# An adaLN block on one core: a new program order on all five engines, the second token half's attention moved among the first feed-forward units, and the output bias folded into the output weights

## The reference

```python
mod = (silu(c) @ wmod).reshape(1, 6, 1, 256)     # c (1, 256)
sa, ca, ga, sb, cb, gb = mod[:, 0], ..., mod[:, 5]
ga, gb = sign(g) * maximum(abs(g), 0.25)         # each
h = layernorm(x) * (1 + ca) + sa                 # x (1, 1024, 256)
x = x + ga * attn(h)
h = layernorm(x) * (1 + cb) + sb
x = x + gb * ffn(h)

def attn(h):
    c = (h @ W_to_kv.T) @ W_compress.T           # 256 -> 64 -> 32
    ch = layernorm(c) * ln_gamma + ln_beta
    q, k, v = ch @ W_q_comp.T, *split(ch @ W_kv_comp.T)
    q, k = rope(q), rope(k)                      # one head of 32
    o = softmax(causal(q @ k.T / sqrt(32))) @ v
    z = o @ W_comp2lat.T
    return z @ W_to_kv + z @ W_out_res.T + b_out_res

def ffn(h):                                      # weights in 4-bit codes with scales
    Wg, Wu, Wd = dequant(...)                    # 2048 x 256 twice, 256 x 2048
    gate, up = h @ Wg.T, h @ Wu.T
    return (gelu_tanh(gate) * up) @ Wd.T
```

## Time and profile before

| | us |
|---|---|
| median of 3 runs | 225.3 |
| lowest, highest | 224.9, 228.08 |
| the profiled execution | 225.71 |
| its span, first to last instruction | 223.9 |
| PE, DVE, POOL, ACT busy in it | 201.6, 138.9, 105.2, 90.6 |
| mean granted TensorE clock, share of 2.4 GHz | 0.942 |

### The profile page before, as it was taken

One profiled execution on the slowest core, in us unless ns is written; L12 is line 12 of the kernel. 1 busy time (PEld: TensorE's weight loads), 2 busy tenths in 40 slices (PEclk: granted clock), 3 DMA queues, 4 the chain that ended last, 5 costly groups with the idle time before them and its releaser, 6 DMA issues. The chain is left out here.

```text
span 223.9 us, 3085 instructions
## 1 busy us (share of the span) xinstructions
PE 201.6 (90%) x1064; PEld 161.6 (72%) x1064; DVE 138.9 (62%) x249; ACT 90.6 (40%) x151; POOL 105.2 (47%) x78
## 2 busy tenths in 40 slices
PE   7998998799867984989999999997989999999991
PEld 2494596584545872868888988886778888888891
DVE  1656864938979789999999512575953333333234
ACT  2001321434176842544364356542343543543320
POOL 4412314506050666496996994660606515515200
PEclk9976975579999999999999999999999999999997
DMA  6999775400000000000000000000020000000002
GB/s 190 329 315 203 181 220 190 162 18 3 0 0 1 0 0 3 1 0 0 1 3 0 0 3 0 0 0 3 0 95 0 0 0 0 3 0 0 0 1 94
DMA packets 5645, 11.31 MB, mean 50 GB/s; under 512 B 544, under 2 KB 2752, under 8 KB 5632
## 3 DMA queue, kind: packets, MB, share of 16 engines
q1 hardware_dynamic: 5216, 10.82, 16.6%
q10 hardware_dynamic: 416, 0.33, 0.5%
HBM read 10.09 MB, written 1.05 MB: 50 GB/s over the span
## 5 line engine op out<-in xcount | busy, mean ns | idle before, releaser
L865 PE MATMUL ps<-H,WS 128*128 128x512 f32 x384 | 95.4, 395 | 8.6 <-DVE wmod_sb L721 5.7
L865 PEld LDWEIGHTS ps<-H,WS 128*128 128x128 f32 x384 | 69.6, 188 | 24.8 <-DVE wmod_sb L721 7.8
L865 PEld LDWEIGHTS ps<-WS,IS 128*128 128x128 f32 x384 | 49.8, 191 | 3.2 <-issue 1.1
L865 PE MATMUL ps<-WS,IS 128*128 128x256 f32 x384 | 51.0, 283 | 0.5 <-DVE wmod_sb L721 0.3
L417 ACT ACTIVATE IS<-wmod_sb 128x512 fp32r<-128x512 f32 x32 | 20.2, 632 | 69.4 <-PE ps L865 39.7
L514 POOL TENSOR_TENSOR WS<-wbuf,WS 128x1024 fp32r<-128x1024 f32 x16 | 39.1, 2441 | 9.8 <-ACT WS L398 9.8
L721 DVE TENSOR_TENSOR wmod_sb<-ps,wmod_sb 128x512 f32<-128x512 f32 x32 | 22.0, 688 | 31.8 <-PE ps L865 25.7
L519 POOL TENSOR_TENSOR WS<-wbuf,WS 128x512 fp32r<-128x512 f32 x16 | 22.4, 1402 | 39.8 <-ACT WS L405 39.8
L282 DVE TENSOR_TENSOR IS<-wmod_sb,IS 128x512 fp32r<-128x512 f32 x18 | 12.8, 710 | 24.4 <-ACT IS L417 23.6
L282 POOL TENSOR_TENSOR IS<-wmod_sb,IS 128x512 fp32r<-128x512 f32 x14 | 21.3, 1529 | 13.7 <-ACT IS L417 11.0
L411 ACT ACTIVATE wmod_sb<-ps 128x512 f32<-128x512 f32 x32 | 18.7, 584 | 5.8 <-PE ps L865 5.8
(11 more groups left out here) (116 smaller groups left out, 209.3 us busy)
## 6 DMA issues: line engine op xcount, KB each, us to landing
wbuf<-packed SPq DMA_DIRECT2D x8, 384.0 KB
wbuf<-scales SPq DMA_DIRECT2D x8, 384.0 KB
xres<-x SPq DMA_DIRECT2D x2, 512.0 KB, 6.2
wmod_sb<-wmod SPq DMA_DIRECT2D x1, 1024.0 KB, 10.4
out<-xres SPq DMA_DIRECT2D x4, 256.0 KB, 2.2
wmod_sb<-wmod SPq DMA_DIRECT2D x1, 512.0 KB, 7.3
rope_sb<-rope SPq DMA_DIRECT2D x1, 512.0 KB, 10.9
cst<-consts SPq DMA_DIRECT2D x1, 322.0 KB, 5.0
```

Source lines behind the costliest of these rows:

```text
L865: return pe.matmul(o, lhsT, rhs, start=start, stop=stop)
```

## The change

Nothing that is computed changes but the places of two factors: the first norm's rsqrt is multiplied in `compress`, behind `project_c`, instead of in `norm1` (now `center1`, which only subtracts the mean); and the bias row is accumulated into the output weights' product on PE, weighted so that it is multiplied by the softmax denominator and divided by it again. `add_bias`, `wsum`, `gab` and the broadcast load of the bias go. x is loaded in three parts, `consts` in two. `full_h0` goes from DVE to ACT, behind both pieces of `H`; the strided read of `norm2` goes into `transpose2`. `residual1` waits for all of its four tiles and interleaves the statistics of the second norm. In the core of the diff below, `for n` is the loop over units.

```diff
 # ACT
 norm1_out(0)
+gate_out()                     # the gb copy, waits for gb_done
 take_bytes(0); v_high(0); qk_high(0); norm1_out(1); take_bytes(1); max_rows(0); exps(0, 0, HT); out_high(0)
+gamma_beta1()                  # the second half's, from DVE
+split_gu(0, 0)
 v_high(1)
-take_bytes(2)
-split_gu(0, 0)
 split_d(0, 0)
 qk_high(1)
-...; max_rows(1)
-exps(1, 0, H0_BLOCK)
 stage_h0()                     # now with both pieces of hfull
-exps(1, H0_BLOCK, 2 * HT - 1); take_bytes(3); split_gu(1, 1); exps(1, 2 * HT - 1, 2 * HT); split_d(1, 1)
 for n in range(UNITS + 2):
-    G = n // 2 + 1
-    if n % 2 == 0 and G > 1: (take_bytes(G + 2)); split_gu(G, G % GROUPS)
+    G = (n + 1) // 2
+    if n % 2 == 0 and n // 2 + 2 < GROUPS: take_bytes(n // 2 + 2)
+    if n % 2: split_gu(G, G % GROUPS)
     gelu(n, n % 2, n >= 2)
-    if n == 0: out_high(1)
     inter_hi(n, n % 2, n >= 2)
-    if n % 2 and G > 1: split_d(G, G % GROUPS)
+    if n % 2: split_d(G, G % GROUPS)
+    if n == 2: max_rows(1); exps(1, 0, 2)
+    elif n == 3: exps(1, 2, 4)
+    elif n == 4: exps(1, 4, 6)
+    elif n == 5: exps(1, 6, 8)
+    elif n == 6: out_high(1)
 # POOL
 low_gu(0, 0, 0); low_d(0, 0, 0); rsqrt(N_LN2)
-for b in range(1, 2 * HT, 2): probs_low(pool, 1, b, b + 1)
-low_gu(1, 1, 1); low_d(1, 1, 1)
 for n in range(POOL_UNITS):
+    G = (n + 1) // 2
+    if n % 2: low_gu(G, G % 2, G)
+    if n == 3: probs_low(pool, 1, 1, 2)
+    elif n == 5: probs_low(pool, 1, 5, 6)
     inter_low(pool, n, n % 2, n >= 2)
+    if n == 3: probs_low(pool, 1, 3, 4)
+    elif n == 5: probs_low(pool, 1, 7, 8)
+    if n % 2: low_d(G, G % 2, G)
...
 # DVE
-    return STEPS_AT_START + 5 * n // 2
+    return 5 * max(0, n - 1) // 2
...
+decode(0)
+probs_low(dve, 0, 0, HT)
 compress(1)
+out_stack(0)
 normc(1)
+residual1(0)
 rotate(1)
 split_v(1)
+norm2(0, range(HT))
 split_qk(1)
+h_low(0, (0, 1))
+decode(1, 0, 3)
 for n in range(UNITS + 2):
     inter_full(n, n % 2, n >= 2)
...
+    if n == 0: decode(1, 3); row_max(1, 0, 4)
+    elif n == 1: row_max(1, 4, len(pieces(1)))
+    elif n == 3: probs_low(dve, 1, 0, 1); probs_low(dve, 1, 2, 3)
+    elif n == 4: probs_low(dve, 1, 4, 5)
+    elif n == 5: probs_low(dve, 1, 6, 7)
+    elif n == 7: out_stack(1)
+    elif n == 8: residual1(1)
+    elif n in (H1_UNIT - 2, H1_UNIT - 1): norm2(1, ...)
     elif n in (H1_UNIT + 1, H1_UNIT + 2): h_low(1, (n - H1_UNIT - 1,))
     decode_more(steps_before(n), steps_before(n + 1))
 # PE
-stay_warm(WC_B, 14)
+stay_warm(WC_B, 10)
...
+project_c(0, (0, 1))
 products(bank(WC_B)[:, 64:64 + DC], ...).then_inc(bias_done, 1)
-project_c(0)
+project_c(0, (2, 3))
 products(bank(GA_B, D), ...).then_inc(ga_done, 1)
-stay_warm(3, 4)
+mod_columns(..., SB, True); mod_columns(..., CB, True).then_inc(modb_done, 1)
 transpose_c(0)
-stay_warm(0, 3)
+products(bank(GB_B, D), ...).then_inc(gb_done, 1)
 project_qkv(0); stack_qk(0); transpose1(1)
-stay_warm(0, 2)
 scores(0, 0, HT)
-(mod_columns SB, CB); project_c(1); max_rows(0); key_scores(0, 0..1); transpose_c(1); key_scores(0, 2, 2)
-attend(0, 0, 0); key_scores(0, 3, 3); stay_warm(4, 3); attend(0, 1..3); project_qkv(1); output(0)
-stay_warm(6, 3); stack_qk(1); stay_warm(4, 10); scores(1, 0, 8); (gb products); max_rows(1); stay_warm(4, 4)
-for b, k in blocks(1): (key_scores, attend, transpose2(0), gate_up(0)); gate_up(1); (last attends)
+project_c(1, (0,)); max_rows(0); project_c(1, (1,)); key_scores(0, 0..2); project_c(1, (2,))
+key_scores(0, 3, 3); attend(0, 0..3); project_c(1, (3,)); stay_warm(4, 2); output(0); stay_warm(4, 2)
+transpose_c(1); project_qkv(1); stay_warm(6, 4); stack_qk(1); transpose2(0)
+gate_up(0, ...); scores(1, 0, 4); gate_up(1, ...); scores(1, 4, 8)
 for n in range(2, UNITS + 3):
     gate_up(n, ...)
-    if n == 2: output(1)
+    if n == 2: max_rows(1)
+    elif n == 3: attend(1, 0, HT); key_scores(1, 3, HT + 3)
+    elif n == 4: attend(1, 2, HT + 2); key_scores(1, 5, HT + 5)
+    elif n == 5: attend(1, 4, HT + 4); key_scores(1, 7, HT + 7)
+    elif n == 6: attend(1, 6, HT + 6)
+    elif n == 7: output(1)
     elif n == H1_UNIT: transpose2(1)
     down(n - 2, ...)
+    if n == 2: key_scores(1, 0..2)
+    elif n == 3: attend(1, 1, HT + 1); key_scores(1, 4, HT + 4)
+    elif n == 4: attend(1, 3, HT + 3); key_scores(1, 6, HT + 6)
+    elif n == 5: attend(1, 5, HT + 5)
+    elif n == 6: attend(1, 7, HT + 7)
```

More of the change, by code:

```diff
@@ L368, in stage_h0 @@
                 for e in range(2):
[L369 to L370 removed]
                     act.activation(H[:, 0, 0, e, :], bank(e), ACT.Identity, bias=mods[:, M_SB + e:M_SB + e + 1],
                                    scale=mods[:, M_CB + e:M_CB + e + 1]).then_inc(h_hi, 1)
+                act.wait_ge(c_done, 2)
+                for e in range(2):
+                    act.activation(hfull[:, e, :], bank(e), ACT.Identity, bias=mods[:, M_SB + e:M_SB + e + 1],
+                                   scale=mods[:, M_CB + e:M_CB + e + 1]).then_inc(h_full, 1)
             def stage_h1(e):
@@ L833, in _ @@
                     inter_low(dve, n, n % 2)
-                if n in (1, 2):
-                    residual1(1, (2 * n - 2, 2 * n - 1))
-                elif n == 3:
-                    stats2(1)
-                elif n in (H1_UNIT - 3, H1_UNIT - 2):
-                    first = 2 * (n - H1_UNIT + 3)
+                if n == 0:
+                    decode(1, 3)
+                    row_max(1, 0, 4)
+                elif n == 1:
+                    row_max(1, 4, len(pieces(1)))
+                elif n == 3:
+                    probs_low(dve, 1, 0, 1)
+                    probs_low(dve, 1, 2, 3)
+                elif n == 4:
+                    probs_low(dve, 1, 4, 5)
+                elif n == 5:
+                    probs_low(dve, 1, 6, 7)
+                elif n == 7:
+                    out_stack(1)
+                elif n == 8:
+                    residual1(1)
+                elif n in (H1_UNIT - 2, H1_UNIT - 1):
+                    first = 2 * (n - H1_UNIT + 2)
                     norm2(1, (first, first + 1))
@@ L1087, in _ @@
             attend(0, 3, 3)
+            project_c(1, (3,))
+            stay_warm(4, 2)
+            output(0)
+            stay_warm(4, 2)
+            transpose_c(1)
             project_qkv(1)
[L1089 to L1090 removed]
+            stay_warm(6, 4)
             stack_qk(1)
[L1092 to L1107 removed]
+            transpose2(0)
+            gate_up(0, 0, 0, 0, 0, first=True, later=False)
+            scores(1, 0, 4)
+            pe.wait_ge(h_full, 2)
             gate_up(1, 0, 0, 0, 1, later=False)
[L1109 to L1110 removed]
+            scores(1, 4, len(pieces(1)))
             for n in range(2, UNITS + 3):
[L1114 removed]
+                gate_up(n, n // 2, n // UNITS, n // 2 % 2, n % 2, first=n == UNITS)
                 if n == 2:
+                    max_rows(1)
+                elif n == 3:
+                    attend(1, 0, HT)
+                    key_scores(1, 3, HT + 3)
+                elif n == 4:
+                    attend(1, 2, HT + 2)
+                    key_scores(1, 5, HT + 5)
+                elif n == 5:
+                    attend(1, 4, HT + 4)
+                    key_scores(1, 7, HT + 7)
+                elif n == 6:
+                    attend(1, 6, HT + 6)
+                elif n == 7:
                     output(1)
@@ L1120, in _ @@
                 down(d, d // 2, d // UNITS, d // 2 % 2, d % 2, first=d % UNITS == 0, last=d == UNITS - 1)
+                if n == 2:
+                    for b in range(3):
+                        key_scores(1, b, HT + b)
+                elif n == 3:
+                    attend(1, 1, HT + 1)
+                    key_scores(1, 4, HT + 4)
+                elif n == 4:
+                    attend(1, 3, HT + 3)
+                    key_scores(1, 6, HT + 6)
+                elif n == 5:
+                    attend(1, 5, HT + 5)
+                elif n == 6:
+                    attend(1, 7, HT + 7)
             with pe.Fori(0, 3) as it:
```

345 lines of the change are left out of this document (152 added, 193 removed).

## The result

The changed kernel takes 250.69 us (median of 4 executions, 249.61 to 252.95) against 225.1 us: 1.11 times as long, 95% interval 1.099 to 1.124. Its profiled execution took 251.63 us, 25.9 more than that of before.

The account below looks back on a forecast made before the run. PE, busy 90%, was taken as nearly saturated only from gate_up(14), after a front chain of small steps and a middle with waits. Front 59.5 + middle 96.15 + rest 81.7 + tail 4.6 + 1.8 = 243.8 us (median 243), range 225 to 256.

Parts of the forecast that it names:

- rsqrt queued behind both low parts, ends 57.2: Front, POOL: second norm's rsqrt waits behind low_gu(0) and low_d(0), ending at 57.2 though its input is there at 52.3.
- half clock throughout: Front: with PE at half clock all through, the summed steps put gate_up(0) at 60.6 us; 59.5 was taken.
- full clock would give 49: Front: every PE step halved, other engines' steps unchanged, puts gate_up(0) near 49 us.
- I(6): End of unit 6's inter product on DVE; 7.05 us after unit 5's, with two loads and four short exps between.
- I(7): End of unit 7's inter product; 5.75 us after unit 6's, for three decode steps, split_gu(4), gelu and inter.
- I(4): End of unit 4's inter product; 11.2 us after unit 3's, through PL(0), attend, down(1), exps and two loads.
- I(10): End of unit 10's inter product; 4.65 us after unit 9's, in units where decode is due one unit before use.
- rival C: Middle: PE gaps of 4 to 5 us drop the clock, half-rate gate_ups in units 6, 8, 10; 250 us, chance 0.10.
- Eight extra loads at 1.28 on the chain: Units 2 to 6, ACT: alternating gelu and exp adds eight table loads of 1.28 us each, 10.3 in all.
- B: Middle, ACT: switching back to exp costs nothing, so 10.3 us less; 233 us, chance 0.10.
- D: Middle, ACT: each table switch also costs a drain of about 1.38 us, 11 more; 254 us, chance 0.02.
- A: Units 2 to 8: the order works as drawn and PE becomes the bound; 217 us, chance 0.12.

Follow-up runs that it names:

- e8_front: Changed kernel with the second norm's rsqrt ahead of group 0's low parts, and transposes, H pieces and norm2 moved earlier; profiled execution 3.46 us shorter.
- a1_front_fillers: Changed kernel with 19 idle matmuls put back on PE in the front; profiled time 6.98 us less, medians 5.1 apart, executions 241.3 to 249.5 us.
- c5_fillers: c3_replanned with out_stack first in the front and idle matmuls there; median 219.37 us, ratio 0.974 to the kernel before the change.
- e2_fill_gaps: Changed kernel with idle matmuls in the three longest PE gaps of the middle; the middle falls by 0.7 us.
- e1_no_switch: Changed kernel with gelu in place of the second half's exps, so eight table loads go; median 248.0 us, middle 5.2 us less.
- e6_batch: Changed kernel with all eight second-half exps in one stretch in unit 2, each block in its own place; profiled time 11.0 us less.
- c1_combined: Changed kernel with e6_batch's exps, e8_front's order and all decoding one unit earlier; median 234.4 us, ratio 1.050 to the kernel before the change.
- c3_replanned: c1_combined with probabilities' low parts on DVE alone, decode re-planned, first exps ahead of inter_hi(2), residual1(1) split; median 230.2 us.

## Why the prediction was right, and where its terms were off

The direction, the place and most terms hold: 243 us forecast, 250.69 measured, inside the range of 225 to 256 and 7.7 above the point. In the profiled execution (243.8 against 251.63) 2.55 of the excess come from the front, 6.09 from units 0 to 13, and 0.8 go off behind gate_up(14). By the prediction's own steps:

- **Front.** gate_up(0) taken at 59.5, came at 62.05. The step "rsqrt queued behind both low parts, ends 57.2" is right to 0.5 us (57.66); e8_front, with three other moves, makes it worth some 1.6 to 2. The sum at half clock throughout had given 60.6, and I took 59.5, below it, where the measured time lies above. Most of the other 1.45 is the 0.46 of the rsqrt, the transposes, which took 1.14 instead of 0.45 at half clock, and 0.25 that they waited behind stack_qk(1) (norm2 ends at 59.08, they start at 59.33). That full clock would give 49 is not shown: a1_front_fillers, in the same order with the clock up for most of the front, came to 55.18, and the 51.77 of c5_fillers has other orders in it.
- **Units 0 to 13.** 96.15 forecast, 102.24 measured. Eight of the twelve terms are within 0.5 us, as to I(2) 14.07 (14.05), I(3) 10.23 (10.05), I(5) 9.95 (9.95) and I(8) 6.50 (6.40); I(6) and I(7) miss by 0.8 and -0.9. The four steps named for I(7) make 4.8 by their own durations, not 5.75; 4.89 was measured. Two terms make up nearly all of the error: I(4), 14.29 against 11.2, and I(10), 7.41 against 4.65, together 5.85 of 6.09. The larger part of both is the clock behind a gap, which e2_fill_gaps shows (12.25 and 4.98 with the clock up); the sum had put it at nothing and left it to rival C. Some 0.9 of I(4) is the low part that took 1.58 us beside POOL instead of 0.7.
- **The loads.** "Eight extra loads at 1.28 on the chain" is right in count and price and wrong in one word: e1_no_switch gives 5.2 to 6.6 us back, not 10.3. The sums along the intervals came out all the same. At I(6), where taking both loads out gave nothing, something else of the same length must stand beside them; no run names it. A sum along a chain gives its length; it does not say that taking a link out shortens it by the link.
- **Rivals.** B (switch back free) falls: the load to exp at 79.36 took 1.28. D (twice the load) falls: 0.02 us on either side. C (half-rate gate_ups 6, 8 and 10: 250) is where the time came out, and its mechanism is there, at down(1) and gate_ups 6 and 10, while gate_up(8) ran at full rate. It came on top of the forecast's loss, not in place of it. That its number fits so well is partly luck: its price was 7.05, of which e2_fill_gaps shows 4.4 on the chain (2.0 and 2.4, none at gate_up(6)), and the front and the low part made up the rest. A (the order works as drawn, 217) falls for this kernel.
- **Behind gate_up(14)**: 80.9 us to the end of PE against 81.7; the tail 4.6 and the 1.8 outside the span as forecast.

So the loss was in the orders, as argued: the experiments that changed orders and left the work in place (e6_batch, then c1_combined and c3_replanned) brought the middle from 105.9 to 84.5 us. These 21.4 us are not all waiting: six loads go with the rounds, and with the gaps goes the half clock behind them, up to 4.4 us by e2_fill_gaps. That it does not reach the 71.8 of before is in part that the kernel before did four of the eight blocks of exps and attends ahead of its gate_up(0); how much else, no run here tells apart.
